# Attention ahead of x1 on VectorE, the second normalised tile behind the scores on TensorE, and ScalarE in step with both

## What is computed

```python
# x: (8, 512, 512), context: (8, 64, 128); 16 heads of 32 channels, 8 experts, the best 2 used
qp = layernorm(x) @ Wq.T
k, v = split(ctx @ Wkv_expand.T)                     # 64 keys per sequence
scores = einsum('bhqd,bhkd->bhqk', qh, kh) / sqrt(32)
scores = where(tril(ones(512, 64)), scores, min)     # only tokens 0 to 62 lose keys
x1 = x + (softmax(scores) @ vh).reshape(...) @ Wout.T
h = layernorm(x1)
logits = h @ router_w.T                              # top 2 of 8, weighted by the logits themselves
moe = sum over the two experts of  logit * (silu(h @ wg) * (h @ wu)) @ wd
shared = silu(h @ sg_w + sg_b) * (h @ su_w + su_b) @ sd_w + sd_b
out = x1 + moe + shared
```

## Time and profile before

| | us |
|---|---|
| median of 3 runs | 845.55 (842.5 to 845.84) |
| the profiled execution, its own time | 844.62 |
| its span in the profile | 842.9 |
| dense stage, first `qT` of step 2 to first entry among the last steps | 42.1 to about 378 |

### The profile page before, as it was taken

How to read it: one execution, slowest core, us unless ns; L and a number is a source line. 1 busy time by engine, 2 the same in 40 slices (tenths; PEclk the granted TensorE clock), 3 DMA queues, 4 the chain that set the end, 5 groups by cost and what they waited for, 6 DMA issues and landing times.

```text
span 842.9 us, 22260 instructions
## 1 busy us (share of the span) xinstructions
PE 787.6 (93%) x7500; PEld 545.4 (65%) x7500; DVE 607.5 (72%) x1196; ACT 439.8 (52%) x805; POOL 428.1 (51%) x530
## 2 busy tenths in 40 slices
PE   4668999999999999989999999999999999999994
PEld 1356777878887888867787877545555555545551
DVE  3878989999999999884468877555555555555552
ACT  2366777777878787866434633333333333333330
POOL 1133876667676767744400010375555666556543
PEclk9679999999999999999999999999999999999997
DMA  8304364635363634255665564698989999889892
GB/s 313 123 27 172 115 211 127 210 125 227 108 233 112 228 106 159 89 158 191 209 211 174 184 224 144 116 165 143 155 144 136 167 143 159 152 146 154 142 146 38
DMA packets 102760, 132.39 MB, mean 157 GB/s; under 512 B 54368, under 2 KB 55392, under 8 KB 101280
## 3 DMA queue, kind: packets, MB, share of 16 engines
q1 hardware_dynamic: 86784, 95.74, 38.5%
q0 software_dynamic: 15904, 35.70, 24.5%
HBM read 71.61 MB, written 52.31 MB: 147 GB/s over the span
## 4 chain that ended last, share of the span: by engine, by line
PE 57%; DVE 10%; issue 6%; DMA 3%; ACT 2%; POOL 2%; SPq 1%; DVEq 0%; POOLq 0%; ACTq 0%
PE psum L1279 38%; PE psum L1327 11%; PE psum L1270 5%; DMA hidT<-xn2T_f 2%; DVE head_max L1007 1%; DVE xy L1020 1%; DVE probsT L860 1%; DVE stats L924 1%; DMA normed_turned<-xn2T 1%; PE psum L1379 1%; DVE xn1T L860 1%; ACT attnT L698 1%; ACT probsT L698 1%; POOL rstd L532 1%; DMA out<-w_q,tabs 1%
## 5 line engine op out<-in xcount | busy, mean ns | idle before, releaser
L678 POOL DMA_INDIRECT out<-w_q,tabs x71 | 112.4, 1584 | 108.6 <-DVE w_q L1259 74.5
L668 POOL DMA_INDIRECT x_in<-normed_tokens,tabs x71 | 70.2, 989 | 132.5 <-DVE tabs L1145 83.9
L1244 DVE SCALAR_TENSOR_TENSOR hid<-psum,tabs,silu_g 128x256 f32<-128x256 f32 x71 | 34.3, 484 | 110.6 <-ACT silu_g L822 109.0
L822 ACT ACTIVATE silu_g<-psum,tabs 128x256 f32<-128x256 f32 x71 | 33.6, 473 | 145.3 <-PE psum L1279 139.1
L1279 PE MATMUL psum<-exp_all,hidT 128*128 x426 | 103.5, 379 | 3.1 <-DMA hidT<-xn2T_f 3.1
L1327 PE MATMUL psum<-xn1T,w_q 128*128 128x128 f16 x1536 | 94.5, 223 | 7.3 <-DVE xn1T L860 7.3
L1279 PE MATMUL psum<-exp_all,probsT 128*128 x420 | 96.4, 379 | 0.0
L1327 PEld LDWEIGHTS psum<-xn1T,w_q 128*128 128x128 f16 x1536 | 89.7, 100 | 7.9 <-DVE xn1T L860 7.6
L1279 PE MATMUL psum<-w_o,attnT 128*128 128x512 f16 x384 | 88.1, 379 | 0.2
L1279 PEld LDWEIGHTS psum<-exp_all,hidT 128*128 128x128 f16 x426 | 41.7, 98 | 54.0 <-issue 5.3
L1259 DVE TENSOR_SCALAR w_q<-psum,y_w 128x512 f32<-128x512 f32 x71 | 53.3, 751 | 21.5 <-PE psum L1279 15.3
(11 more groups left out here) (199 smaller groups left out, 1706.2 us busy)
## 6 DMA issues: line engine op xcount, KB each, us to landing
x_in<-x SPq DMA_DIRECT2D x64, 256.0 KB, 3.1
exp_all<-experts SPq DMA_DIRECT2D x8, 1536.0 KB, 8.5
out<-xy SPq DMA_DIRECT2D x32, 256.0 KB, 2.1
normed_tokens<-xn SPq DMA_DIRECT2D x32, 256.0 KB, 2.4
normed_turned<-xn2T SPq DMA_DIRECT2D x32, 256.0 KB, 2.0
w_q<-out SPq DMA_DIRECT2D x32, 256.0 KB, 3.2
out<-w_q SPq DMA_DIRECT2D x32, 256.0 KB, 2.9
probsT<-normed_turned SPq DMA_DIRECT2D x16, 256.0 KB, 3.4
```

What stands on the lines that cost most here:

```text
L668: pool.indirect_dma_start(x_in[:, t % 4, :], None, xn_dram, bass.IndirectOffsetOnAxis(gather_at[:, t:t + 1], 0)).then_inc(gathered[t % 4], 16)
L678: pool.indirect_dma_start(out, bass.IndirectOffsetOnAxis(add_at[:, t:t + 1], 0), y[:, t % Y_RING, :], None, bounds_check=TOKENS - 1, oob_i ...
```

## The change

No operation is added, removed or resized, and POOL and SP keep their order. Three engines run the same instructions of a dense step in another order:

- **DVE.** A step began with the statistics of x, then `qT` low. Now `qT` low comes first, then `join_stats(1, t5)`, which is the old `join_stats(1, t4)` put off into the next step, then the statistics of x, `attnT` low, `join_stats(0)`. The expert's magnitudes stand behind `xn1T` low, no longer behind `qT` low. At the end of a step the reciprocal and `attn` (t3) come ahead of `x1` and its statistics (t4).
- **PE.** The four transposes of `xn2` stand behind the scores, no longer ahead of them.
- **ACT.** `xn2` (t5) stands behind `xn1T` high, no longer ahead of `attnT` high. `xn2T` high and `xn2T_f` stand behind `xn1`, no longer ahead of it.

```diff
@@ ACT step @@
-                if live(t5):
-                    act.wait_ge(ln_rstd[1], t5 + 1)
-                    wait(act, xn2_stored[(j + 1) % 2], 16 * (TPB // 2 * b + (j - 5) // 2))
-                    act.activation(xn2[:, (j + 1) % 2, 0:H], x1, ACT.Identity, bias=rstd[:, 1, 2:3],
-                                   scale=rstd[:, 1, 1:2]).then_inc(xn2_ready, 1)
                 if live(t4):
                     act.wait_ge(attnT_mm, t4 + 1)
                     copy(flat(attnT[:, 0, :, :]), bank(4), 1.0, attnT_hi)
...
                     copy(flat(xn1T[:, 0, :, :]), bank(7), X_UP, xn1T_hi)
                 if live(t5):
-                    act.wait_ge(xn2T_mm, t5 + 1)
-                    wait(act, xT_stored, 16 * t5)
-                    copy(flat(xn2T[:, 0, :, :]), bank(6), X_UP, xn2T_hi)
-                if live(t5):
-                    wait(act, xn2T_ready, t5)
-                    copy(xn2T_f[:, :], bank(6), X_UP, xn2T_hi)
+                    act.wait_ge(ln_rstd[1], t5 + 1)
+                    wait(act, xn2_stored[(j + 1) % 2], 16 * (TPB // 2 * b + (j - 5) // 2))
+                    act.activation(xn2[:, (j + 1) % 2, 0:H], x1, ACT.Identity, bias=rstd[:, 1, 2:3],
+                                   scale=rstd[:, 1, 1:2]).then_inc(xn2_ready, 1)
...
                     act.activation(xn1[:, :], x_in[:, j % 2, 0:H], ACT.Identity, bias=rstd[:, 0, 2:3],
                                    scale=rstd[:, 0, 1:2]).then_inc(xn1_ready, 1)
+                if live(t5):
+                    act.wait_ge(xn2T_mm, t5 + 1)
+                    wait(act, xT_stored, 16 * t5)
+                    copy(flat(xn2T[:, 0, :, :]), bank(6), X_UP, xn2T_hi)
+                if live(t5):
+                    wait(act, xn2T_ready, t5)
+                    copy(xn2T_f[:, :], bank(6), X_UP, xn2T_hi)
@@ DVE step @@
+                if live(t2):
+                    dve.wait_ge(qT_hi, t2 + 1)
+                    low(flat(qT[:, 1, :, :]), bank(5), Q_DOWN, flat(qT[:, 0, :, :]), qT_ready)
+                if live(t5):
+                    join_stats(1, t5)
                 if live(tile):
                     dve.wait_ge(xa_loaded[j % 2], 16 * (TPB // 2 * b + j // 2 + 1))
                     stage_stats(0, x_in[:, j % 2, 0:H], tile)
-                if live(tile):
-                    join_stats(0, tile)
-                if live(t2):
-                    dve.wait_ge(qT_hi, t2 + 1)
-                    low(flat(qT[:, 1, :, :]), bank(5), Q_DOWN, flat(qT[:, 0, :, :]), qT_ready)
-                if e is not None and j in ((1, 2, 3) if isinstance(b, int) and b == 0 else (0, 2, 3)):
-                    expert_magnitudes(e, max(0, j - 1))
...
                                       ALU.subtract).then_inc(attnT_ready, 1)
+                if live(tile):
+                    join_stats(0, tile)
...
+                if e is not None and j in ((1, 2, 3) if isinstance(b, int) and b == 0 else (0, 2, 3)):
+                    expert_magnitudes(e, max(0, j - 1))
                 entry_amid(tile, entry)
...
                     dve.tensor_tensor(probs[:, :, :], scores, head_max[:, :, None].to_broadcast([P, NH, SK]),
                                       ALU.subtract).then_inc(shifted, 1)
+                if live(t3):
+
+                    dve.wait_ge(av_mm, t3 + 1)
...
+                if live(t3):
+                    dve.wait_ge(recip_ready, t3 + 1)
+                    wait(dve, attnT_mm, t3)
...
                 if live(t4):
 
                     dve.wait_ge(proj_mm, t4 + 1)
...
-                if live(t4):
-                    join_stats(1, t4)
@@ PE step @@
-                if live(t5):
-                    pe.wait_ge(xn2_ready, t5 + 1)
-                    wait(pe, logits_ready, t5)
-                    transposes(bank(6), xn2[:, (j + 1) % 2, :], C, xn2T_mm)
                 entry_amid(tile, entry)
...
                     last.then_inc(scores_mm, 1)
+                if live(t5):
+                    pe.wait_ge(xn2_ready, t5 + 1)
+                    wait(pe, logits_ready, t5)
+                    transposes(bank(6), xn2[:, (j + 1) % 2, :], C, xn2T_mm)
```

More of the change, by code:

```diff
@@ L967, in step @@
                 tile = TPB * b + j
-                t1, t2, t3, t4 = [tile - n for n in range(1, 5)]
+                t1, t2, t3, t4, t5 = [tile - n for n in range(1, 6)]
                 e = found(b)
                 scaled = found(b - 1) if j == 1 else None
+                if live(t2):
[3 more added lines that the diff above has]
+                    join_stats(1, t5)
                 if live(tile):
@@ L973, in step @@
                     stage_stats(0, x_in[:, j % 2, 0:H], tile)
-                if live(tile):
-                    join_stats(0, tile)
-                if live(t2):
-                    dve.wait_ge(qT_hi, t2 + 1)
-                    low(flat(qT[:, 1, :, :]), bank(5), Q_DOWN, flat(qT[:, 0, :, :]), qT_ready)
-                if e is not None and j in ((1, 2, 3) if isinstance(b, int) and b == 0 else (0, 2, 3)):
-                    expert_magnitudes(e, max(0, j - 1))
-                if scaled is not None:
-                    expert_scales(scaled, 0)
                 if live(t4):
@@ L986, in step @@
                                       ALU.subtract).then_inc(attnT_ready, 1)
+                if live(tile):
+                    join_stats(0, tile)
                 if scaled is not None:
-                    expert_scales(scaled, 1)
+                    expert_scales(scaled, 0)
                 if live(t3):
@@ L994, in step @@
                 if scaled is not None:
-                    expert_scales(scaled, 2)
+                    expert_scales(scaled, 1)
                 if live(t1):
@@ L1008, in step @@
                 if scaled is not None:
-                    expert_scales(scaled, 4)
+                    expert_scales(scaled, 3)
                 if live(t2):
@@ L1013, in step @@
                                       ALU.subtract).then_inc(shifted, 1)
+                if live(t3):
+                    dve.wait_ge(av_mm, t3 + 1)
+                    av = psum[:, 0:2, 0:4 * 2 * VW].rearrange("p n (q w) -> p n q w", w=VW)
+                    dve.reciprocal(recip[:, :].rearrange("p (n q) -> p n q", n=2), av[:, :, :, HD]).then_inc(recip_ready, 1)
+                if scaled is not None:
+                    expert_scales(scaled, 4)
+                if live(t3):
+                    dve.wait_ge(recip_ready, t3 + 1)
+                    wait(dve, attnT_mm, t3)
+                    dve.tensor_tensor(attn[:, :, :].rearrange("p (n q) d -> p n q d", n=2), av[:, :, :, 0:HD],
+                                      recip[:, :].rearrange("p (n q) -> p n q", n=2)[:, :, :, None].to_broadcast(
+                                          [P, 2, NH // 2, HD]), ALU.mult).then_inc(attn_ready, 1)
                 if live(t4):
@@ L1025, in step @@
                     expert_scales(scaled, 5)
-                if live(t3):
-                    dve.wait_ge(av_mm, t3 + 1)
-                    av = psum[:, 0:2, 0:4 * 2 * VW].rearrange("p n (q w) -> p n q w", w=VW)
-                    dve.reciprocal(recip[:, :].rearrange("p (n q) -> p n q", n=2), av[:, :, :, HD]).then_inc(recip_ready, 1)
-                if live(t4):
-                    join_stats(1, t4)
-                if live(t3):
-                    dve.wait_ge(recip_ready, t3 + 1)
-                    wait(dve, attnT_mm, t3)
-                    dve.tensor_tensor(attn[:, :, :].rearrange("p (n q) d -> p n q d", n=2), av[:, :, :, 0:HD],
-                                      recip[:, :].rearrange("p (n q) -> p n q", n=2)[:, :, :, None].to_broadcast(
-                                          [P, 2, NH // 2, HD]), ALU.mult).then_inc(attn_ready, 1)
                 if isinstance(b, int) and (b, j) == (0, 0):
```

2 lines of the change are left out of this document (1 added, 1 removed).

## The result

The changed kernel takes 904.12 us (median of 4 runs, 902.74 to 905.81), the kernel before 844.02 us (4 runs, 839.87 to 845.84). The ratio is 1.072, 95% interval 1.0672 to 1.0769: slower by 7%. 908 us was predicted. The profiled execution took 903.48 us with a span of 901.8, 58.9 above the span before.

What follows compares the result with a forecast made beforehand. The prediction took a circle of waits over POOL to bound the loop, 49.6 us a batch for 40.68. Terms of +48.8, +12.2, +0.3 and +2 made +63.3 on 844.62, so 908 us, range 882 to 930.

Steps and rivals of the forecast that it cites:

- The circle: Loop steps with pieces: X, join, POOL's deviations with base and piece between, ACT's xn1 and queue, next X; 12.9 us; 80%.
- X: The time of ACT's qT high in a loop step, from which the prediction counts what follows.
- queue: ACT's work from xn1 to the next X: xn1, xn2T high, xn2T_f, two piece pairs and Exp; 5.38 us.
- the piece wait: ACT's second piece pair waits until POOL has split the first: 0.7 us more.
- The step without pieces: Loop step j = 1, held by PE, which waits 0.65 us for xn2: 10.5 us.
- The key copies: POOL's copies from j = 1 end 3.05 us behind the next X; inv_std(1) is 1.55 late, j = 2 takes 13.3.
- Steps 6 to 8 with POOL's extra weights: The extra weights, 2.27 us each, lie in the circle three times: 45.9 us for 33.71, +12.2.
- Other edits: Earlier attn and attnT low can take back at most 1.1 us a batch, which the circle swallows.
- The drain: Behind the loop, transposes of xn2 and ACT's SiLU stand later: +2 us, bounded by nothing and 8.
- The start: The stretch from the start to step 6: about 0, with +0.3 us for step 5.
- Signs: ACT's xn1 waits 2 to 3.5 us for POOL; wrong if xn1 before X + 5 or base not following X.
- The clock rival: PE's clock falls to 1.2 GHz for a third of its work in a step: 927 us, up to 960; chance 7%.

Runs made afterwards that it cites:

- e1: The changed kernel with the join of x1's statistics put back to the end of DVE's own step: 859.25 us, ratio 1.021 to the kernel before.
- e2: The kernel before with only the join of x1's statistics moved behind qT low of the next step: 935.7 us, ratio 1.108.
- e3: The changed kernel with POOL computing base twice, same result: 946.84 us, ratio 1.123 to the kernel before.
- e6: The changed kernel with POOL making both deviations first, then base, and the second piece at the step's end: 862.45 us, ratio 1.023.
- e11: The changed kernel with the expert's magnitudes alone put back ahead of attnT low: 903.74 us, ratio 1.072 to the kernel before.
- e7: The kernel before with the changed orders of ACT and PE, DVE as before: 851.58 us, ratio 1.012.
- e5: The kernel before with DVE reading the expert's magnitudes behind xn1T low, nothing else changed: 854.81 us, ratio 1.017.

## Why the prediction was right, point by point

- **The circle and its terms.** Measured after X in the step shown above: join done at 1.38 (I had 1.45), base at 2.91 (3.0), the first deviation's start at 5.38 (5.48), xn1 at 6.76 (6.86), then a queue of 5.99 (5.38 + 0.7 = 6.08) with the piece wait at 0.71. The steps are 10.65, 13.03, 12.79 and 12.75 for 10.5, 13.3, 12.9 and 12.9 predicted. e1 and e2 show that the join does it, e3 and e6 that the circle runs over POOL, e11 that it does not run over the magnitudes.
- **The step without pieces** is held by PE's wait for xn2, 10.65 for 10.5. xn2 starts at X + 3.08 (I had 3.03); PE is free earlier than I took, at X + 2.84 for 3.2, and waits 1.11 us for 0.65. e6, where xn1 no longer holds any step, has 10.6 to 10.7 in three of four.
- **The key copies** delay j = 2, a little less than I took: the second deviation starts at X + 3.06 (3.2) and xn1 at X + 7.10 (7.27).
- **Steps 6 to 8 with POOL's extra weights**: +11.9 for +12.2, but the agreement is luck. By my terms the steps were to be 15.6, 15.2 and 15.2 us; they are 13.78, 16.78 and 15.04. In step 6 the last key copy ends at X + 1.6, not 3.05, so the second deviation starts early and xn1 with it. Step 7 is ended by PE, not by ACT's queue. `av` stands for 3.56 us until POOL has copied the values, which it does behind the first deviation, and then the clock is low:

```profile
104.61 0.81 ACT L767 ACTIVATE xn<-x_in,rstd 128x512 f32<-128x512 f32 x1 [5.19 <-POOL rstd L536]
...
106.28 1.48 PE L1398 MATMUL psum<-kv_store,probsT 128*128 128x66 f16 x24 [3.56 <-POOL kv_store L576]
...
112.39 0.60 ACT L698 ACTIVATE qT<-psum 128x512 f16<-128x512 f32 x1 [2.01 <-PE psum L1327]
```

  The stretch behind that wait (clock third from the end) has a clock of 0.56, and `av` and the queries take 6.07 us in it, where the same matmuls take 3.57 in step 16 (220.38 to 223.95):

```profile
106.28:112.39 6.11, 6.11 (x80) 6.11 (x81) 2.30 (x4) 3.70 (x6) 2.31 (x2) 0.56 0.14 46
```

  ACT was through with its queue at 110.39, so the low clock cost 2.0 us of this step.
- **Other edits at nothing.** In the changed kernel right for the magnitudes (e11); the place of `attn` was not tested there. In themselves they are not free, though: e7 costs 1.2%, e5 1.7%. I wrote that the magnitudes' move could only take back waiting; e5 shows a loss of 2.2 us a batch, hidden here.
- **The drain** was mis-sized, +4.8 for +2, of which 3.1 lie ahead of the routing matmuls (line 1418) and 1.7 behind, where the work is unchanged.
- **The start** gained 4.7 where I had nothing. The same early instructions start their second tile anywhere from 37.4 to 42.1 us from one kernel to the next, so I cannot put it down to the change. This miss and the drain's are of opposite sign and leave 2 us in the sum.
- **Signs.** The wait for xn1 was to be 2 to 3.5 us in every step: in the loop it is 2.87 in three and 1.85 in j = 2, where xn2 itself comes late. xn1 starts no earlier than X + 6.76 and base follows X, so neither sign of being wrong appeared. That POOL would wait less for DVE's moments was wrong. It waits more, 136.8 us over the kernel for 87.8, and 3.18 us at a time in the step shown, since it has caught up with its queue when the late join comes. PE's share in the loop fell to 84%, where I said about 80%.
- **The clock rival** did not take place in the loop of the changed kernel, where the clock is 1.00 in every batch and PE's waits are 1.55 us at most in step 8 and 1.34 behind it, the stretches with missing records left aside. It did take place in step 7, as told above. e2 shows what it can cost, at pauses of 2 us. The Trainium skill, "TensorE: Matmul & The Clock Gate", section "Part 1: The HAM clock gate", says that activity lifts the throttle. e2's rows agree only in part: the clock fell to 0.52 and 0.58 behind stretches in which PE was busy for 2.09 of 4.01 and 0.85 of 2.90 us, but the last section shows one in which it did not.

## What to carry to other kernels

Before an instruction is moved past a wait, write down for each engine what comes behind it until the same place is reached one step later. If the chain closes and is longer than the work of the busiest engine, its length is the step: 0.18 us of DVE work, moved behind one instruction that waits for ACT, cost 45 us. Costs of moves do not add. The same part cost 2.2 us a batch in one order, nothing in another and had the other sign in a third, so a part must be priced in the order in which it will stand. And a late producer should be set where its consumer engine has other work ready: with PE's wait for xn2 ahead of the scores (e2) the same late join cost about 8 us a batch at full clock and 12 as measured, with it behind them about 6 (e1 against the changed kernel). ACT's and DVE's orders differ as well between these two pairs.
